# The top-2 routing of a mixture of experts, moved ahead of a barrier and in between normalization steps

## The reference, cut to what matters

```python
def _L0_attn_ref(x, Wq, Wv, Wo, Wg, ln_gamma, ln_beta, beta):
    q = (x @ Wq.T).reshape(Bsz, Ls, NHEAD, HEAD_DIM)
    v = (x @ Wv.T).reshape(Bsz, Ls, NHEAD, HEAD_DIM)
    ret = _retention_scan(v, lam)
    out = (q * ret).reshape(Bsz, Ls, D)
    out = _layernorm(out, ln_gamma, ln_beta)
    return (out * jax.nn.silu(x @ Wg.T)) @ Wo.T

def _L0_ffn_ref(hidden_states, Wg, W1, W2, W3, bias):
    routing_weights = jax.nn.sigmoid((x @ Wg.T).astype(jnp.float32))
    scores = routing_weights + bias
    _, top_k_index = jax.lax.top_k(scores, 2)
    top_k_weights = jnp.take_along_axis(routing_weights, top_k_index, axis=1)
    top_k_weights = top_k_weights / top_k_weights.sum(axis=-1, keepdims=True)
    one_hot = jax.nn.one_hot(top_k_index, Wg.shape[0], dtype=x.dtype)
    expert_w = jnp.einsum('tk,tke->te', top_k_weights, one_hot)
    h1 = jnp.einsum('th,efh->tef', x, W1)
    h3 = jnp.einsum('th,efh->tef', x, W3)
    g = jax.nn.silu(h1) * h3 * expert_w[:, :, None]
    return jnp.einsum('tef,ehf->th', g, W2)

x = _layernorm(x + _L0_attn_ref(x, ...))
x = _layernorm(x + _L0_ffn_ref(x, ...))
```

## Time and profile before

| | us |
|---|---|
| median of 3 runs | 4671.31 (4669.36 to 4671.64) |
| the profiled execution | 4667.79 |
| its span, slowest core (core 6) | 4666.2 |
| spans of the 8 cores | 4656.8 to 4666.2 |
| TensorE busy | 3966.2 (85%) |
| VectorE busy | 1159.1 (25%) |
| ScalarE busy | 350.4 (8%) |
| GpSimd busy | 318.0 (7%) |

### The profile page before, as it was taken

One profiled execution on the slowest core, in us unless ns is written; L12 is line 12 of the kernel. 1 busy time (PEld: TensorE's weight loads), 2 busy tenths in 40 slices (PEclk: granted clock), 3 DMA queues, 4 the chain that ended last, 5 costly groups with the idle time before them and its releaser, 6 DMA issues.

```text
span 4666.2 us, 46275 instructions; the slowest of 8 cores (4656.8 to 4666.2 us)
## 1 busy us (share of the span) xinstructions
PE 3966.2 (85%) x17125; PEld 1698.2 (36%) x17465; DVE 1159.1 (25%) x2036; ACT 350.4 (8%) x621; POOL 318.0 (7%) x602
## 2 busy tenths in 40 slices
PE   5699837499999999999959983749999999999994
PEld 1243312144444444444414330214444444444441
DVE  0122061421211211201262207142121121121126
ACT  0002100000000000000010210100000000000001
POOL 2100000000000000000100000000000000000000
PEclk6699959699999999999979995979999999999997
DMA  9843316344744344444454331635454434434442
GB/s 160 136 75 59 63 38 151 99 76 73 133 82 73 68 76 71 67 77 71 74 122 77 61 65 22 147 103 87 71 124 86 73 68 76 71 68 77 73 69 76
DMA packets 136778, 389.00 MB, mean 83 GB/s; under 512 B 15728, under 2 KB 23920, under 8 KB 136560
## 3 DMA queue, kind: packets, MB, share of 16 engines
q0 software_dynamic: 85392, 302.06, 39.0%
q1 hardware_dynamic: 32736, 58.78, 4.1%
q10 hardware_dynamic: 18432, 25.17, 1.6%
HBM read 646.03 MB, written 41.94 MB: 147 GB/s over the span
## 4 chain that ended last, share of the span: by engine, by line
PE 79%; DVE 9%; DMA 5%; issue 4%; ACT 2%; POOL 0%; DVEq 0%; ACTq 0%; POOLq 0%; PEldq 0%; SPq 0%
PE ps L970 19%; PE ps L988 19%; PE ps L1069 19%; PE ps L709 5%; PE ps L635 5%; PE ps L497 5%; PE ps L568 5%; DMA wring<-xpre 2%; DVE gbufS L1049 2%; DVE ntmpS L669 1%; DVE ygS L677 1%; DVE ot2S L1158 1%; DVE rstdR L424 1%; DVE ntmpS L663 1%; ACT sqS L760 1%
## 5 line engine op out<-in xcount | busy, mean ns | idle before, releaser
L1069 PE MATMUL ps<-gbufS,wring 128*128 128x512 bf16 x4016 | 920.6, 388 | 38.3 <-DVE gbufS L1049 33.7
L970 PE MATMUL ps<-xnS,wring 128*128 128x512 bf16 x4008 | 919.1, 385 | 14.3 <-DMA wring<-w1T 8.3
L988 PE MATMUL ps<-xnS,wring 128*128 128x512 bf16 x4016 | 900.1, 379 | 4.0
L1069 PEld LDWEIGHTS ps<-gbufS,wring 128*128 128x128 bf16 x4096 | 405.7, 99 | 556.6 <-issue 96.8
L970 PEld LDWEIGHTS ps<-xnS,wring 128*128 128x128 bf16 x4096 | 403.9, 99 | 510.6 <-issue 44.2
L988 PEld LDWEIGHTS ps<-xnS,wring 128*128 128x128 bf16 x4096 | 400.7, 98 | 483.4
L1009 DVE TENSOR_TENSOR gbufS<-ps,sh1S 128x512 bf16<-128x512 f32 x256 | 165.0, 686 | 1510.8 <-PE ps L988 1299.7
L709 PE MATMUL ps<-ygS,wring 128*128 128x512 bf16 x1000 | 268.3, 425 | 123.1 <-DVE ygS L677 120.8
L1003 ACT ACTIVATE sh1S<-ps 128x512 bf16<-128x512 f32 x256 | 138.9, 595 | 2409.7 <-PE ps L970 2389.0
L497 PE MATMUL ps<-xnS,wring 128*128 128x512 bf16 x1005 | 230.2, 385 | 54.8 <-ACT vS L524 38.4
L1094 DVE SCALAR_TENSOR_TENSOR x2S<-ps,x2S 128x512 f32<-128x512 f32 x192 | 132.8, 692 | 527.6 <-PE ps L1069 522.1
(11 more groups left out here) (134 smaller groups left out, 1442.5 us busy)
## 6 DMA issues: line engine op xcount, KB each, us to landing
wring<-w1T POOLq DMA_DIRECT2D x128, 512.0 KB, 6.1
wring<-w3T POOLq DMA_DIRECT2D x128, 512.0 KB, 6.0
wring<-w2T POOLq DMA_DIRECT2D x128, 512.0 KB, 6.1
wring<-xpre POOLq DMA_DIRECT2D x48, 512.0 KB, 9.9
xf32S<-xfm SPq DMA_DIRECT2D x64, 256.0 KB, 7.3
wring<-wvT POOLq DMA_DIRECT2D x32, 512.0 KB, 6.0
wring<-wqT POOLq DMA_DIRECT2D x32, 512.0 KB, 6.1
wring<-wgT POOLq DMA_DIRECT2D x32, 512.0 KB, 5.7
```

The costliest lines, as they stand in the source:

```text
L970: g1 = pr.step("pe", lambda en, kt=kt, c=c, slot=slot1: en.matmul(out=psS[c][:, 0:CW], lhsT=wringS[slot][:, kt * P:(kt + 1) * P], rhs=x1nS ...
L988: g3 = pr.step("pe", lambda en, kt=kt, c=c, slot=slot3: en.matmul(out=psS[2 + c][:, 0:CW], lhsT=wringS[slot][:, kt * P:(kt + 1) * P], rhs= ...
L1069: grp = pr.step("pe", lambda en, k=k, c=c, slot=slot2: en.matmul(out=psS[4 + c][:, 0:CW], lhsT=wringS[slot][:, k * P:(k + 1) * P], rhs=gbu ...
```

## The change

Four things are done:

- The router scores (L855 to L878) are computed ahead of the normalization instead of behind the barrier.
- `emit_router_front(tt)` is called in the normalization loop, after blocks kt = 1, 3, ..., 15 for tt = 0, 1, ..., 7, and no longer in the loop of the first expert.
- `ewtS` becomes [128, 64], 8 columns for each tt, and the wait of a front for the back before it goes.
- `emit_router_back(tt)` stays where it was, behind the matmuls of ft = tt in the first expert.

```diff
-    ewtS = A("ewtS", [P, E], F32)
+    ewtS = A("ewtS", [P, 8 * E], F32)
...
             bt2 = ln_rows_bcast(st2_sum + st2_sq, 4, 6, 2, 3)
 
-            t_mbb = pr.tick("dve", lambda en: en.tensor_copy(
-                out=muBb[:, 0:TH], in_=muB[:, 0:TH]), deps=bt2 + muB_b.begin_write() * 0)
...
-            for kt in range(KT):
-                xcslot, xcbuf = xcR.next()
...
-            pr.barrier()
-            for b in psB:
-                b.ready = None
-                b.readers = []
...
             for c in range(NCW):
                 psB[c].wrote(rl_grp[c])
...
-                trw = pr.tick("dve", lambda en: en.tensor_tensor(
-                    out=ewtS[:, 0:E], in0=sctS[:, 0:E], in1=fbB[:, 0:E],
-                    op=ALU.subtract), deps=[tev, t_fbB] + ew_done[-1:])
+                trw = pr.tick("dve", lambda en, tt=tt: en.tensor_tensor(
+                    out=ewtS[:, tt * E:(tt + 1) * E], in0=sctS[:, 0:E],
+                    in1=fbB[:, 0:E],
+                    op=ALU.subtract), deps=[tev, t_fbB])
...
+            t_mbb = pr.tick("dve", lambda en: en.tensor_copy(
+                out=muBb[:, 0:TH], in_=muB[:, 0:TH]), deps=bt2 + muB_b.begin_write() * 0)
...
+            for kt in range(KT):
+                xcslot, xcbuf = xcR.next()
...
+                if kt % 2 == 1 and kt // 2 < TT:
+                    emit_router_front(kt // 2)
...
+            pr.barrier()
...
                     for ft in range(FT):
-                        if first_expert and ft < TT:
-                            emit_router_front(ft)
                         slot1, wb1, tld1 = load_wcol(
                             w1_d[e, ft].rearrange("p kt m -> p (kt m)"))
...
-                    if first_expert:
-                        for tt in range(FT, TT):
-                            emit_router_front(tt)
-                            emit_router_back(tt)
-                        first_expert = False
+                    first_expert = False
```

More of the change, by code:

```diff
@@ L829, in emit_half @@
-            t_x1nw_all = [(f"dA{k}", pr.counts[f"dA{k}"]) for k in range(2)]
-            pr.barrier()
-            for b in psB:
-                b.ready = None
-                b.readers = []
[L836 to L849, removed]
@@ L910, in emit_router_front @@
                     scalar2=None, op0=ALU.is_equal), deps=[tif, t_io8])
-                tw1 = pr.tick("dve", lambda en: en.scalar_tensor_tensor(
+                tw1 = pr.tick("dve", lambda en, tt=tt: en.scalar_tensor_tensor(
                     out=rt_jnk[:], in0=rt_oh1[:], scalar=1.0,
-                    in1=ewtS[:, 0:E], op0=ALU.mult, op1=ALU.mult,
+                    in1=ewtS[:, tt * E:(tt + 1) * E], op0=ALU.mult, op1=ALU.mult,
                     accum_out=rt_w1[:]), deps=[to1, trw])
-                tw2 = pr.tick("dve", lambda en: en.scalar_tensor_tensor(
+                tw2 = pr.tick("dve", lambda en, tt=tt: en.scalar_tensor_tensor(
                     out=rt_jnk[:], in0=rt_oh2[:], scalar=1.0,
-                    in1=ewtS[:, 0:E], op0=ALU.mult, op1=ALU.mult,
+                    in1=ewtS[:, tt * E:(tt + 1) * E], op0=ALU.mult, op1=ALU.mult,
                     accum_out=rt_w2[:]), deps=[to2, trw, tw1])
@@ L929, in emit_router_front @@
                     deps=[tri, tn1])
-                te1 = pr.tick("dve", lambda en: en.tensor_scalar(
-                    out=ewtS[:, 0:E], in0=rt_oh1[:],
+                te1 = pr.tick("dve", lambda en, tt=tt: en.tensor_scalar(
+                    out=ewtS[:, tt * E:(tt + 1) * E], in0=rt_oh1[:],
                     scalar1=rt_w1[:, 0:1], scalar2=None, op0=ALU.mult),
                     deps=[tn1, trw])
-                te2 = pr.tick("dve", lambda en: en.scalar_tensor_tensor(
-                    out=ewtS[:, 0:E], in0=rt_oh2[:], scalar=rt_w2[:, 0:1],
-                    in1=ewtS[:, 0:E], op0=ALU.mult, op1=ALU.add),
+                te2 = pr.tick("dve", lambda en, tt=tt: en.scalar_tensor_tensor(
+                    out=ewtS[:, tt * E:(tt + 1) * E], in0=rt_oh2[:],
+                    scalar=rt_w2[:, 0:1],
+                    in1=ewtS[:, tt * E:(tt + 1) * E], op0=ALU.mult, op1=ALU.add),
                     deps=[tn2, te1])
@@ L942, in emit_router_back @@
                 d7 = psB[7].begin_write()
-                ttb = pr.tick("pe", lambda en: en.transpose(
-                    out=psS[7][0:E, 0:P], in_=ewtS[:, 0:E],
+                ttb = pr.tick("pe", lambda en, tt=tt: en.transpose(
+                    out=psS[7][0:E, 0:P], in_=ewtS[:, tt * E:(tt + 1) * E],
                     identity=identf[:, :]), deps=[te2, t_id] + d7)
@@ L951, in emit_router_back @@
                 ew_done.append(tee)
+            rt_state = {"ew_done": ew_done, "back": emit_router_back}
+            t_mbb = pr.tick("dve", lambda en: en.tensor_copy(
+                out=muBb[:, 0:TH], in_=muB[:, 0:TH]), deps=bt2 + muB_b.begin_write() * 0)
+            muB_b.read(t_mbb)
+            t_rbb = pr.tick("dve", lambda en: en.tensor_copy(
+                out=rstdBb[:, 0:TH], in_=rstdB[:, 0:TH]), deps=bt2)
+            rstdB_b.read(t_rbb)
+            xn_war = g_grp[NH - 1]
+            x1n_tok = {}
@@ new lines, in emit_half @@
+            for kt in range(KT):
+                xcslot, xcbuf = xcR.next()
+                trb = pr.dma("sp", lambda en, kt=kt, xcslot=xcslot: en.dma_start(
+                    out=xcS[:, xcslot * TH:(xcslot + 1) * TH],
+                    in_=x1bhbm[kt * P:(kt + 1) * P, hoff:hoff + TH]),
+                    deps=t_x1bw_all + xcbuf.begin_write(), sem=f"dC{xcslot}")
+                xcbuf.wrote(trb)
+                for c in range(NCW):
+                    ntslot, ntbuf = ntbR.next()
+                    tn1 = pr.tick("dve", lambda en, xcslot=xcslot, c=c, ntslot=ntslot: en.tensor_tensor(
+                        out=ntbS[:, ntslot * CW:(ntslot + 1) * CW],
+                        in0=xcS[:, xcslot * TH + c * CW:xcslot * TH + (c + 1) * CW],
+                        in1=muBb[:, c * CW:(c + 1) * CW], op=ALU.subtract),
+                        deps=[trb, t_mbb] + ntbuf.begin_write())
+                    muB_b.read(tn1)
+                    xcbuf.read(tn1)
+                    tn2 = pr.tick("dve", lambda en, kt=kt, c=c, ntslot=ntslot: en.tensor_tensor(
+                        out=xnS[:, kt * TH + c * CW:kt * TH + (c + 1) * CW],
+                        in0=ntbS[:, ntslot * CW:(ntslot + 1) * CW],
+                        in1=rstdBb[:, c * CW:(c + 1) * CW],
+                        op=ALU.mult),
+                        deps=[tn1, t_rbb, xn_war])
+                    rstdB_b.read(tn2)
+                    ntbuf.wrote(tn1)
+                    ntbuf.read(tn2)
+                    x1n_tok[(kt, c)] = tn2
+                    xn_b.wrote(tn2)
+                if kt % 2 == 1 and kt // 2 < TT:
+                    emit_router_front(kt // 2)
@@ new lines, in emit_half @@
+            t_x1nw_all = [(f"dA{k}", pr.counts[f"dA{k}"]) for k in range(2)]
+            pr.barrier()
+            for b in psB:
+                b.ready = None
+                b.readers = []
+        with (
+            nc.sbuf_tensor(f"gbufS{half}", [P, 2 * FT * TH], BF16) as gbufS,
+            nc.sbuf_tensor(f"x2S{half}", [P, KT * TH], F32) as x2S,
+            nc.sbuf_tensor(f"sh1S{half}", [P, 4 * CW], BF16) as sh1S,
+            nc.sbuf_tensor(f"ot2S{half}", [P, 4 * CW], F32) as ot2S,
+        ):
+            xrbS = xf32S
+            xrR = xfR
+            x1nS = xnS
+            t_x1n = [None] * KT
+            for kt in range(KT):
+                toks = [x1n_tok[(kt, c)] for c in range(NCW)]
+                t_x1n[kt] = max(toks, key=lambda t: t[1])
+            ew_done = rt_state["ew_done"]
+            emit_router_back = rt_state["back"]
```

## The result

The changed kernel takes 4723.35 us against 4671.48 us (medians of 6 runs each), 1.0112 of the kernel before with a 95% interval of 1.0096 to 1.0128: slower by 52 us, where 55.4 were forecast. The profiled execution took 4720.65 us.

The account below looks back on a forecast made before the run. It took VectorE's list to bound the normalization, where TensorE idles. Scores, fronts and saved transposes, 5.6 + 23.1 + 5.5 + 23.3 - 2.1 = 55.4 us, made the median 4726.7 us, 1.2% slower; range 4716 to 4738.

Parts of the forecast that it names:

- The stretch and what bounds it: Normalization up to the barrier, TensorE idle: added VectorE work lengthens the program; VectorE's small instructions in the first expert cost nothing.
- The room: VectorE's waits for loads in the normalization, 5.5 us a half, vanish when fronts are added.
- A front: Each router front in the normalization costs VectorE a 3.58 us chain; the stage grows by 23.1 and 23.3 us.
- One sign: Expected trace mark: first to last normalization step takes 56 us in each half.
- The scores: Router scores ahead of the normalization, with nothing beside them on VectorE, add 5.6 and 5.5 us in the two halves.
- The saving behind the barrier: Moving the scores from behind the barrier saves nothing; the first weight load still takes as long.
- its cover: First w1 load behind the barrier outlasts the router by 4 to 5 us; without it, removal saves up to 5.6 a half.
- TensorE in the first expert: The scores' transpose goes from between matmul blocks: 14 x 0.15 = 2.1 us saved, bounds 0 and 3.2.
- A: Fronts in the normalization close up to the distance of independent instructions, 1.35 us each: +19.8 us, time 4691; chance 4%.
- B: First weights behind the barrier land sooner because VectorE is idle there: 6.6 us saved, time 4720; chance 8%.
- C: Not slower: fronts fall into the normalization's waits for loads, leaving +9.0 us, 4680; chance 2%.
- D: Something unseen costs more, as fronts always stalling 0.46 us and the clock rising late: +13 us, time 4740; chance 5%.

Follow-up runs that it names:

- the scores alone: Changed kernel with the eight fronts put back into the first expert, only the router scores ahead of the normalization: 1.0019 of the kernel before.
- four fronts: Changed kernel with fronts 0 to 3 in the normalization and 4 to 7 back in the first expert: 1.0078 of the kernel before.
- the third slot: Kernel before with three slots in xcS instead of two: 1.0007 of the kernel before (0.995 to 1.0065).
- the early loads: First four weight blocks loaded ahead of the normalization: 0.9999 in the kernel before; 1.0108 and 1.0073 in the changed kernel, all against the kernel before.
- matmuls in the normalization: Kernel before with block 0's w1 and w3 groups ahead of the barrier, scores and fronts one block later: 0.9931 and 0.9911 of the kernel before.

## Why the prediction was right

**The stretch and what bounds it.** Right. Work that VectorE got in the stretch in which TensorE idles came out nearly one for one, and its removal from the first expert gave nothing back on VectorE's side. The runs with the scores alone (+9 us by the ratio, 2 to 15 by its interval; 11 forecast) and with four fronts (+36, 25 to 48; 33 forecast) show it by parts.

**The room.** Right: 5.5 us a half taken from the two paces, 5.1 and 5.2 measured by the third slot (33.2 to 28.1, 33.0 to 27.7, core 6 of the one trace and core 0 of the other; 4.7 and 5.6 as means of the 8 cores). The 7.7 us of waits in the earlier trace rows are 3.9 a half and would have been too little: that view leaves out short waits.

**A front.** Right, 3.64 us where 3.58 were taken; the stalls of 0.5 us that I let cancel against the overlap do occur there too. From first step to issue of the weights the sum was off by +0.7 and -0.6 us. One sign was worded wrongly: from the first to the last step it takes 52.8 and 52.5 us, and 56 only with the eighth front, which stands behind the last step.

**The scores.** Right in the first half (5.5 for 5.6), 0.3 short in the second, where the wait for ACT is 1.11 us instead of 0.83.

**The saving behind the barrier.** Right that it is nothing: issue to first matmul stayed at 8.5 to 9 us in the mean. What its cover was, the early loads show.

**TensorE in the first expert.** Mis-sized: the term of 2.1 us measured 3.7. I took only the 0.15 us between L886 and the matmul. But the transpose of the weights ahead of it also lets go sooner. TensorE in the kernel before, core 6:

```profile
1000.43 0.27 PE L943 MATMUL ps<-identf,ewtS 128*8 128x128 f32 x1
1000.64 0.23 PE L886 MATMUL ps<-identf,r8a 8*128 8x8 f32 x1
1000.80 7.08 PE L970 MATMUL ps<-xnS,wring 128*128 128x512 bf16 x32
```

From L943 to the matmul it took 0.37 us, and now L888 to L979 takes 0.11. The gain of a block is 0.26 us. The 3.7 lie outside even the bound of 3.2 that the prediction gave for this term; at 1.6 us they could not move the whole out of its range.

**The rivals.** A is out: the fronts keep their chain between independent steps, 0.26 us from L834 to L838 where it was 0.27. The Trainium skill's 58 cycles per instruction (VectorE: DVE Perf Modes, "The TRN2 errata") remain far under what a chain of small instructions costs here; the same section gives about 150 cycles as the measured fixed term, an estimate of 0.16 us for 8 elements, which fits the duration of one such instruction (0.17 us at 900.38) but not the distance to the next that needs it. B is out: with VectorE idle behind the barrier, the first load took 8.8 and 8.5 us in the mean of the cores, against 8.6 and 9.0, and 9.2 and 9.8 with the scores alone moved. B had also misread: the first L855 of each half ended before the first load was issued (917.86 against 918.09, 3150.23 against 3150.27), so only the second ran beside issues, those of later loads. The Trainium skill's rule on GpSimd and VectorE (SBUF — State Buffer, "Who interferes with whom") was therefore not put to a test by the first load; on its landing nothing of it is seen. C is out by the four fronts and by the wait rows. D did not occur: four of 16 fronts stalled, not all, and the clock behind the stretch cost between -0.2 and +0.5 us a half.

## What to carry to other kernels

The average of an engine says nothing on where its work is free: VectorE was busy for a quarter of the span, and the 35 us in which everyone waited for it were a place where more of it costs in full. Ahead of moving work off one wait, look at what else ends there at the same time; here the load behind the barrier hid the router, and only with the load gone did moving the scores bring the first matmul forward, by less than they cost on VectorE. A stretch that idles one engine is to be filled with that engine's work: 64 matmuls cost less than 2 us there (on core 2 the barrier came 3.0 us behind the last step instead of 1.3), as against 3.6 us for the 15 small VectorE instructions of one front. When TensorE's work is moved, look at the clock just behind: here it stood at 0.50 when the next full group began, which gave some 2.6 us of the gain back.

## What was not expected of the hardware

The first weight load behind the barrier took from 7.4 to 10.8 us until the matmul on different cores and halves of one execution before, and from 7.0 to 11.0 in the changed kernel, with nothing seen in the traces that tells the cores apart. Here it is in the run with the scores alone, core 7:

```profile
927.61 0.53 POOL L234 DMA_DIRECT2D wring<-w1T  x1 [116.63 <-PEq L65]
...
937.38 1.01 PE L979 MATMUL ps<-xnS,wring 128*128 128x512 bf16 x2 [9.65 <-DMA wring<-w1T]
```

I took the slowest core's 9.1 and 9.7 us, and a forecast on it is good to 2 us a half at best. And two transposes in a row on TensorE cost more than the two apart: 0.37 us until the next matmul, where the back transpose alone takes 0.11 and the front's alone 0.15 or 0.16 (936.31 to 936.47 in the run with matmuls in the normalization).
